# High halves of y of the odd fc1 blocks made by GpSimd instead of VectorE, their low halves by VectorE two slots further behind

## The reference

```python
h = (x - mu) * jax.lax.rsqrt(var + EPS) * ln_gamma + ln_beta
y = jax.nn.silu(h.reshape(-1, H) @ w1 + fc1_bias)      # H = 512, F = 2048
z = y @ w2 + fc2_bias
ffn = residual + 0.5 * z
out = x + attn(xn) * silu(ffn)
```

## Time and profile before

| what | value |
|---|---|
| median of 3 runs | 1266.86 us (1266.81 to 1268.67) |
| profiled execution, its own time | 1264.73 us |
| its span in the trace | 1262.8 us |
| PE busy | 1190.5 us, 94% |
| DVE busy | 1143.2 us, 91% |
| ACT busy | 914.7 us, 72% |
| POOL busy | 784.3 us, 62% |
| granted TensorE clock, mean | 0.993 of full speed |

### The profile page before, as it was taken

The page is one execution under the profiler, slowest core; times in us unless marked ns, Lnnn a source line. Parts: engine busy times, 40 slices in busy tenths (PEclk is TensorE's granted clock), DMA queues, the critical chain, the costliest instruction groups (busy, mean ns, idle before and its releaser), DMA issues.

```text
span 1262.8 us, 18949 instructions
## 1 busy us (share of the span) xinstructions
PE 1190.5 (94%) x6028; PEld 616.7 (49%) x6028; DVE 1143.2 (91%) x1969; ACT 914.7 (72%) x1590; POOL 784.3 (62%) x760
## 2 busy tenths in 40 slices
PE   2799999999999999999999999999999999999994
PEld 1344554555555555555555545555455545555551
DVE  8889989899998999999899998989999899999897
ACT  6788776777777767676777777677777776768672
POOL 4076847569474765947477494756947476594642
PEclk9999999999999999999999999999999999999997
DMA  9511120302112030210303012030211203020011
GB/s 331 172 44 35 46 55 3 99 1 67 35 34 68 1 101 1 68 34 19 82 1 92 10 54 48 6 96 1 67 34 36 66 1 100 1 67 1 22 47 35
DMA packets 41620, 65.68 MB, mean 52 GB/s; under 512 B 11696, under 2 KB 11952, under 8 KB 41008
## 3 DMA queue, kind: packets, MB, share of 16 engines
q1 hardware_dynamic: 41232, 64.36, 18.7%
q10 hardware_dynamic: 288, 0.08, 0.0%
HBM read 47.59 MB, written 16.81 MB: 51 GB/s over the span
## 4 chain that ended last, share of the span: by engine, by line
PE 73%; DVE 12%; ACT 8%; issue 5%; POOL 1%; DMA 1%; SPq 0%; ACTq 0%; DVEq 0%
PE blk L490 27%; PE blk L508 25%; PE side L450 6%; DVE blk L776 5%; PE side L475 4%; PE side L439 3%; ACT blk L636 3%; PE side L467 2%; DVE y_split L767 2%; DVE tops L814 2%; ACT z_rows L662 1%; PE side L426 1%; DVE y_split L762 1%; PE side L468 1%; PE side L469 1%
## 5 line engine op out<-in xcount | busy, mean ns | idle before, releaser
L776 DVE TENSOR_TENSOR blk<-blk,ratio_rows 128x512 f32<-128x512 f32 x960 | 646.0, 692 | 79.4 <-PE blk L508 75.8
L636 ACT ACTIVATE blk<-blk,ratio 128x512 f32<-128x512 f32 x768 | 508.2, 666 | 228.9 <-PE blk L490 222.8
L490 PE MATMUL blk<-h_split,q_sb 128*128 128x512 f16 x2048 | 611.1, 380 | 12.1 <-ACT y_full L643 4.2
L508 PE MATMUL blk<-w_sb,y_split 128*128 128x512 f16 x2048 | 608.7, 379 | 2.5 <-POOL w_sb L1081 1.3
L508 PEld LDWEIGHTS blk<-w_sb,y_split 128*128 128x128 f16 x2048 | 199.4, 98 | 247.4 <-DVE blk L776 7.3
L490 PEld LDWEIGHTS blk<-h_split,q_sb 128*128 128x128 f16 x2048 | 194.4, 98 | 224.1 <-ACT blk L636 32.5
L643 ACT ACTIVATE y_full<-blk,par,last 128x512 f32<-128x512 f32 x256 | 201.6, 787 | 82.6 <-PE blk L490 81.9
L767 DVE SCALAR_TENSOR_TENSOR y_split<-y_full,up,y_split 128x512 f16<-128x512 f32 x256 | 220.6, 862 | 0.1
L1072 POOL CAST h_split<-h_full 128x512 f16<-128x512 f32 x64 | 52.6, 822 | 239.8 <-ACT h_full L592 239.8
L762 DVE TENSOR_SCALAR y_split<-y_full,up 128x512 f16<-128x512 f32 x256 | 170.1, 665 | 0.0
L1060 POOL TENSOR_SCALAR g_rows<-xt,mv,gs 128x512 f32<-128x512 f32 x60 | 133.1, 2227 | 0.0
(11 more groups left out here) (153 smaller groups left out, 1087.9 us busy)
## 6 DMA issues: line engine op xcount, KB each, us to landing
xt<-in_x SPq DMA_DIRECT2D x64, 256.0 KB, 4.6
x_again<-in_x SPq DMA_DIRECT2D x256, 64.0 KB, 1.9
out<-z_rows SPq DMA_DIRECT2D x256, 64.0 KB, 1.7
w_sb<-in_q SPq DMA_DIRECT2D x4, 1024.0 KB, 14.2
ratio_rows<-ratio_dram SPq DMA_DIRECT2D x4, 1024.0 KB, 7.3
y_split<-in_q SPq DMA_DIRECT2D x1, 1024.0 KB, 10.2
h_split<-in_q SPq DMA_DIRECT2D x1, 1024.0 KB, 12.5
z_rows<-in_q SPq DMA_DIRECT2D x1, 1024.0 KB, 13.9
```

The lines of the kernel that those rows point to most:

```text
L490: mm = pe.matmul(blk[J % 2][:], q1_sb[:, g, j // 4, w, j % 4 * P:(j % 4 + 1) * P], a[:, c % 2, g, :], start=(g == 0 and n == 0), stop=(g = ...
L508: mm = pe.matmul(blk2[:, i, :], y[:, J % Y_RING, rows], w2_sb[:, j, part, :], start=(j == 0 and n == 0), stop=(j == FB - 1 and n == len(te ...
L636: act.activation(blk[J % 2][:], blk[J % 2][:], ACT.Copy, scale=ratio1[:, at:at + 1]).then_inc(blk_scaled, 1)
L776: dve.tensor_tensor(blk2[:, i, :], blk2[:, i, :], ratio2_rows[:, j, :], ALU.mult).then_inc(blk2_scaled, 1)
```

## The change

DVE no longer has y_high of odd blocks: POOL makes it, at the same slots e = 4, 12, 20, ..., ahead of its other pieces of the slot, as a multiplication by the scale and by 1.0. A semaphore of its own tells y_low of it, and one more tells POOL that the scale is there. y_low of odd blocks moves from two slots behind the last fc1 step to four, from e = 5, 13, 21, ... to e = 7, 15, 23, ..., and stands there behind y_high of the even block. The 128 y_high and 128 y_low of even blocks stay as they are, and so do PE's and ACT's instructions.

```diff
-MASK_LAG, MEM_LAG, GLOW_LAG, YHIGH_LAG, YLOW_LAG = 1, 1, 3, 1, 2
+MASK_LAG, MEM_LAG, GLOW_LAG, YHIGH_LAG, YLOW_LAG, ODD_YLOW_LAG = 1, 1, 3, 1, 2, 4
...
             def y_low(J):
-                dve.wait_ge(y_hi_done, J + 1)
+                if J % 2:
+                    dve.wait_ge(y_hi_odd_done, J // 2 + 1)
+                else:
+                    dve.wait_ge(y_hi_done, J // 2 + 1)
...
+            dve.tensor_copy(branch_end[:], up_y).then_inc(y_scale, 1)
...
-                if (at := fc1_step(G - YHIGH_LAG) if G >= YHIGH_LAG else None) and at[1] == KC - 1:
+                if (at := fc1_step(G - YHIGH_LAG) if G >= YHIGH_LAG else None) and at[1] == KC - 1 and at[0] % 2 == 0:
                     y_high(at[0])
-                if (at := fc1_step(G - YLOW_LAG) if G >= YLOW_LAG else None) and at[1] == KC - 1:
+                if (at := fc1_step(G - YLOW_LAG) if G >= YLOW_LAG else None) and at[1] == KC - 1 and at[0] % 2 == 0:
+                    y_low(at[0])
+                if (at := fc1_step(G - ODD_YLOW_LAG) if G >= ODD_YLOW_LAG else None) and at[1] == KC - 1 and at[0] % 2:
                     y_low(at[0])
...
+            def odd_y_high(J):
+                if J == 1:
+                    pool.wait_ge(y_scale, 1)
+                wait(pool, blk2_done, NT * (J - Y_RING + 1))
+                pool.wait_ge(silu_done, J + 1)
+                pool.tensor_scalar(y_hi[:, J % Y_RING, :], y_full[:, J % 2, :], up_y, 1.0, ALU.mult, ALU.mult
+                                   ).then_inc(y_hi_odd_done, 1)
...
             for G in range(SLOTS):
                 c, e = divmod(G, STEPS)
+                if (at := fc1_step(G - YHIGH_LAG) if G >= YHIGH_LAG else None) and at[1] == KC - 1 and at[0] % 2:
+                    odd_y_high(at[0])
```

More of the change, by code:

```diff
@@ L279, in build @@
         silu_done = sem("silu_done")
-        y_hi_done = sem("y_hi_done")
+        y_hi_done, y_hi_odd_done, y_scale = sem("y_hi_done"), sem("y_hi_odd_done"), sem("y_scale")
         y_lo_done = sem("y_lo_done")
```

## The result

| what | before | after |
|---|---|---|
| median | 1266.86 us | 1291.14 us (1291.08 to 1295.61, 4 runs) |
| ratio to before | | 1.0199, 95% interval 1.0187 to 1.0212 |
| profiled execution, its own time | 1264.73 us | 1291.08 us |
| span | 1262.8 us | 1289.3 us |

The changed kernel is 2.0% slower: 24.3 us by the medians, 26.4 us by the profiled executions. The forecast was 13.8 us on that second scale.

A forecast was written before the change was run, and what follows sets the result against it. PE was taken to lose time where DVE reaches masks and g_low late behind bunched work. 1264.73 + 15 chunks x 1.00 - 1.2 in the tail, chunk 0 nothing, gave 1278.5 us; range 1257 to 1300, the forecast's own 1269 to 1290.

The forecast's parts named there:

- the tail: After the chunks, where DVE leads: three y_high leave DVE's chain, -1.2 us.
- What bounds the kernel: PE's waits before read and turn jobs end with DVE; what counts is DVE's work since last level with PE.
- The bunching: Moved y_low stands beside even y_high and y_low, right ahead of masks and g_low: PE late by 1.00 us per chunk.
- Slot 33: Mask at e = 33, counted from the pair of e = 31: later by 0.46 to 0.88 us, taken as 0.65, all lost.
- Slot 57: g_low at e = 57, counted from the pair of e = 55: later by 0.19 us, at a turn where PE waits.
- slots 9: Mask at e = 9, counted from the pair of e = 7 at the free y_low price: later by 0.19 us.
- Slot 21: Mask at e = 21: y_high(20) goes, y_low(15) comes in at 1.08; net -0.03 us, bounds -0.45 and +0.46.
- POOL's price: Each new y_high on POOL taken as 0.95 us, range 0.76 to 2.22; in time up to about 1.2.
- dear rival: Odd y_high costs 1.51 us or more on POOL, so DVE stands still in y_low: 1292 to 1300 us; chance 0.18.
- The faster rival: y operations between e = 15 and 24 meet POOL less, the 0.86 at e = 23 is given back: 1257 us; chance 0.17.
- The scale: The forecast time is on the profiled execution's scale; the median before was 2.1 us above that, and this was left out.
- the signs named: DVE busy falls 60 to 85 us, POOL's rises about 120; mask at e = 33 starts 3.9 to 4.4 behind the pair.

The follow-up runs named there:

- second kernel of part 8: Kernel before with only POOL's last output piece moved from slot 30 to slot 37: 1268.05 us, ratio 1.0007.
- Parts 1, 5 and 6: All y_high on DVE, only odd y_low moved: 1301.63 us; changed kernel with y_low(27) or y_low(51) back at two slots: 1277.94, 1286.70 us; both back: 1269.19 us.
- part 8: Changed kernel with POOL's last output piece moved from slot 30 to slot 37, behind the y_high of e = 36: 1279.46 us, ratio 1.0086.
- Part 2: Changed kernel with odd y_low back at two slots, odd y_high still on POOL: 1275.16 us, ratio 1.0063 to the kernel before.
- part 7: Kernel before, but POOL makes y_high of odd blocks except those of e = 12 and 28, and y_low(19) stands in slot 25: 1261.47 us, ratio 0.9964.
- first kernel of part 7: Kernel before, but POOL makes only the y_high of e = 20, and that block's y_low stands in slot 25: 1265.76 us, ratio 0.9992.

## Why the prediction was off in size

Losses of PE per chunk, in us, before and after from the timelines:

| place | forecast | measured |
|---|---|---|
| read, e = 11 | +0.19 | +0.24 |
| read, e = 23 | -0.03 | -0.41 |
| wo, e = 26 | 0 | +0.58 in 8 of 14 chunks, 0.33 on average |
| read, e = 35 | +0.65 | +1.03 |
| turn, e = 59 | +0.19 | +0.44 |
| sum | +1.00 | +1.63 |

By the starts of PE's matmuls each of the 14 middle chunks is 1.67 us longer on average, 23.3 us in sum. The last one, which has no turns, is 1.0 longer, chunk 0 is 2.0 longer (forecast nothing), and the tail gives nothing (forecast -1.2). That makes 26.3 of the 26.4 us between the profiled executions.

The 2.0 of chunk 0 can't be put down to the change. The second kernel of part 8 has the same program as the kernel before in chunk 0, and its chunk 0 took 2.5 us longer in its profiled execution. The granted clock differed there too: from 20 to 32 and 32 to 60 us of the span it was 1.00 and 0.94 in the kernel before, 0.68 and 0.83 in the changed one, 0.71 and 0.82 in that of part 8. Without chunk 0 the sum is 24.4 us, the difference of the medians; against the 13.8 forecast that is what has to be explained.

- **What bounds the kernel**: right. PE's losses end with DVE, at masks, at g_low and (new) at `remember`, and DVE's total says nothing: it fell by 36.3 us while the kernel grew.
- **The bunching**: the edit and the places were right. Parts 1, 5 and 6 show that the move is the loss and that slots 33 and 57 carry most of it. What the bunch costs by its length alone is less. At e = 11, where no y operation is held, it is 0.24. At e = 35 it is 0.10 over the kernel before (part 8), which has a hold of 0.42 there itself; the other 0.93 of the +1.03 go with the hold.
- **Slot 33, the step that failed.** The prediction put y_high(31) at 0.40 and split the surcharge over the two y_low, by whether POOL is busy in that stretch: 0.60 + 0.40 + 0.87 + 0.60 + 1.08 + 0.60. The row has 0.60 + 1.33 + 0.67 + 0.60 + 0.66 + 0.60: y_high, which the prediction took as free, was held, and both y_low, which it took as dear, were free. The sum of 4.15 became 4.46, and the loss +1.03 where +0.65 was forecast (the middle of its own two bounds is 0.67). The price of a y operation is not an average over a stretch; it is fixed by which POOL operation is running when it starts, and part 8 shows that by taking that one away. The rule of the Trainium skill's page "SBUF — State Buffer", section "SBUF: two separate sides", by which the prediction worked out +1.44 for this slot, was set aside because no y_low was over 1.65 long. The measured +1.03 lies between the two numbers, and the rule had the mechanism: a wait for the running operation's end. The trace of before had it too: y_low(32) of the earlier trace rows ends at 531.03 + 1.16 = 532.19, which is 0.55 behind the end of POOL's output operation, 531.64:

```profile
530.13 1.51 POOL L1119 TENSOR_TENSOR z_rows<-z_rows,x_again 128x512 f32<-128x512 f32 x1
```

- **Slot 57**: 0.25 too small, 0.20 of it by the same step. y_high(55) was 0.56 and y_low(56) 0.86 long, beside POOL's split of h, which I had not looked at. The other 0.05 is missing at slots 9 and 33 as well: DVE starts block2_out about 0.04 behind the end of the pair, and the count let it start at once.
- **Slot 21**: a gain of 0.41 rather than 0.03. The price of 1.08 for the moved y_low was too low here (1.67), but y_low(16) fell out of its hold (1.16 long before, 0.74 after) and y_high(15) was held for less (1.42, 0.91), and these gave back more.
- **remember**: the `wo` job of e = 26 was in no term of the sum, and no reason was given for leaving it out. A y_low more (of the block ending at e = 19) stands ahead of `remember` in slot 23 and is held; where y_high(23) is held too, PE loses 0.58.
- **POOL's price**: 0.69 us against 0.95, below even the lower end of 0.76, and like L1102 rather than L1145. The dear rival was wrong: DVE never waited for POOL. Part 2 shows that it does at lag 2, for up to 3 us.
- **The faster rival**: its mechanism was real, since the wait at e = 23 did shrink by half. It was outweighed at the other places.
- **The scale**: the 2.1 us between the profiled execution and the median of before were left out; after, the two agree to 0.1 us. As in the sum above, this is about what chunk 0 differs by.
- Of the signs named: DVE's busy time fell by 36 us and not 60 to 85, POOL's rose by 66 and not 120 (128 x 0.69 = 88, and its other operations are 22 shorter in sum); the mask of e = 33 stands 4.50 behind the pair, just over the 3.9 to 4.4.

## What to carry to other kernels

Look for the moments at which the follower engine is level with the one it serves, and count only what stands between such a moment and its next deadline; a relief ahead of it is worth nothing, and a move across it costs its full length and any hold that it brings on. List every deadline of the engine, those that cost nothing today too, since the third wait here came from one. When work goes from VectorE to GpSimd, lay the two engines' timelines over each other: each VectorE operation of a kind that can be held costs the rest of the GpSimd operation that it meets, and moving one GpSimd piece out of a bunch gave the changed kernel 12 us (part 8), while taking 128 operations off VectorE gave 10.5 (the changed kernel against that of part 1). In the kernel before, the same move gave nothing, because the piece met a y operation again at its new moment.

## What the runs showed of the hardware

- A y operation of VectorE that starts while GpSimd runs a two-input operation or a cast of 128 x 512 ends 0.28 us (one tensor input) or 0.55 us (two) behind the end of that one, to within 0.01 us, in all 241 cases counted above that began more than 0.2 us ahead of that end. Beside a tensor-scalar operation of GpSimd 77 of the 105 that began that early were free; the other 28, all y_high in the last half microsecond of a normalise, end 0.28 us behind it. Why those were held, no run here tells.
- A y_high that starts 0.03 to 0.04 us ahead of a two-input GpSimd operation can be held by it as well: 8 of 14 in the middle chunks of the changed kernel were; one that started 0.10 ahead (part 7) was not, nor were 14 y_low of the changed kernel that started 0.04 ahead of L1120.
- block2_out, which has one input in PSUM, stays at 0.69 us beside all of them.
- It goes the other way too: L1139 of GpSimd was 1.27 us long in the first kernel of part 7, where it started ahead of y_high(28), and 1.52 us in the third, where it met the running y_high.
- A GpSimd multiply by two scalars with f16 output, 128 x 512, is 0.69 us, less than half of the single multiplication L1145 in the earlier trace rows (1.51, float32 out).
